# Keys of the next batch in cross attention: three context buffers, and the key sums ahead of a value product

## Chip, cores, metric

One core of a Trainium2 chip runs one launch of the kernel. The metric is the time of the device in microseconds (us), less is better. TensorE is called PE here, VectorE DVE, ScalarE ACT, GpSimd POOL, and SP is the engine that issues the transfers. PEld is the load of PE's weights.

## What is computed

A decoder layer with three parts, each followed by a layer norm, for 16 batches of 100 rows of 512: causal self attention with 16 heads, cross attention, and a routed feed-forward with two of eight experts. The change lies in the cross attention, whose computation is this (hidden is x, encoder is the context of 361 rows per batch):

```python
q = (hidden_states @ Wq + bq).reshape(b, s, 16, 128).transpose(0, 2, 1, 3)
k = (encoder_hidden_states @ Wk + bk).reshape(b, se, 4, 128).transpose(0, 2, 1, 3)
v = (encoder_hidden_states @ Wv + bv).reshape(b, se, 4, 128).transpose(0, 2, 1, 3)
q = _rmsnorm(q, qn_w)      # over the 128 of a head
k = _rmsnorm(k, kn_w)
scores = jnp.einsum('bhsd,bhed->bhse', q, k_of_its_group) / sqrt(128) + mask
out = softmax(scores) @ v_of_its_group
return out @ Wo
```

There are 16 query heads and 4 key and value heads, so 4 query heads share one key head.

## The kernel before

The kernel is written engine by engine: each engine has its own program of instructions in a fixed order, and semaphores tie them together (`wait_ge`, `then_inc`). Nothing is reordered by a scheduler. Three phases follow each other: self attention with the query projection, cross attention (`cross_attention_phase`), and the experts. All products are float32 products made of three float32r ones, high times high, high times low and low times high (`product3`, whose matmuls all carry line 75). An operand therefore has to be split: ACT copies it to the high half, and DVE or POOL subtracts that to get the low half.

The cross attention runs `body(j)` for batches j = 0 to 15 and then once more for what is left over. A batch has four groups s = 0 to 3, one per key head, and each engine walks through them. In group s PE does, for h = 0, 1, 2: the scores of query head h (3 matmuls, line 75, b_q with b_kTh and b_kTl), the transposes of one third of the probabilities of the group before (line 951), and a `quarter`, which is a piece of other work. Then come the scores of head 3, a fourth quarter, more pieces, and the product of the values with the probabilities of the group before (`values_product`). What the pieces are:

- Group 0: the output projection of the batch before, its third group of heads, as quarters (one query head each); the values of this batch (`values(j, 0)` ahead of the value product, 1 and 2 behind it).
- Group 1: the output projection of the batch before, its fourth group of heads, as quarters; then `keys(j + 1, 0)`, the first key head of the next batch. It waits for all three context pieces of that batch to be split (`ctx_lo`).
- Group 2: `keys` 1 and 2 in the quarters, `keys` 3 behind them, one head of the output projection; the value product; then `key_sums` (line 987), which sums the squares of the four key heads with a matrix of ones.
- Group 3: output projection in the quarters and around the value product.

The context of a batch is three pieces of 121 rows. SP loads each (`load_ctx`, line 863) to one of two raw buffers `ctxr[:, c % 2]`, so that the third waits for the low half of the first. ACT makes the high half (`context_hi`, line 1113) in group 1, one behind each of the first three exponents, and POOL the low half (`context_lo`, line 1404).

A key head goes through: DVE adds the bias (`key_bias`, line 1215), ACT squares (`key_square`, line 1094), PE sums, ACT takes logarithm, exponential and square (`key_root`, lines 1100 to 1104), DVE makes a Newton step (`key_newton`, lines 1221 and 1224), SP writes the four rows of roots to memory and loads them back spread over 128 partitions (`spread_key_roots`, lines 878 and 882, tensor b_krb), DVE scales (`key_scale`, line 1229), ACT and DVE split (lines 1108 and 1233). The root stands at the start of ACT's group 3, the Newton step behind the first probabilities in DVE's group 3, and the scaling of key head 0 in the middle of it:

```python
if now:
    queries(n + 1)
    if s == 3 and not last:
        key_scale(j + 1, 0)
    masked(j, s, 3)
    invert_sums(j, s, 0)
    if s == 3 and not last:
        keys_lo(j + 1, 0)
    invert_sums(j, s, 2)
```

`masked` (line 1250) reads the scores of a head and writes them with the mask and their maximum, ACT's `exponent` (line 1126) follows, and `invert_sums` (line 1256) releases POOL, which in `normalise` scales heads 0 and 1 of the group (line 1420, behind the small line 1399), makes the low half of the queries of the next group (`queries_lo`, line 1409), and scales heads 2 and 3. The first scores of a group wait for that low half (`q_lo`) and for the split key (`kt_lo`), its first transpose for all four scaled heads (`p_rdy`). Evictions to SBUF of the attention output are `b_oTh` (ACT, line 1190) and `b_oTl` (DVE, line 1326).

Keys have buffers for two batches of four heads (`[P, 2, XKV, SEP + 1]`), the squares share memory with the high halves and the raw keys with the low ones.

## Time and profile before

| what | value |
|---|---|
| median of 3 runs | 1666.06 us (1663.55 to 1667.65) |
| the profiled execution, its own time | 1665.94 us |
| span in its trace | 1663.6 us |
| PE busy | 1460.4 us (88%) |
| DVE, ACT, POOL busy | 855.6, 800.2, 509.1 us |

The profile is one execution. Its times are read as: start, duration, engine, line, operation, what is written and what is read, and in brackets how long the engine stood idle in front of it and what released it. A matmul's duration holds its passage through the array, so that matmuls behind each other start closer together than they last. "Granted clock" (PEclk) is the share of the full 2.4 GHz that PE was given; 0.50 is 1.2 GHz.

The cross attention fills the stretch from about 447 to 1446 us of the span.

### The profile page before, as it was taken

How to read it: one execution, taken by the hardware profiler on the slowest of the kernel's cores; microseconds unless marked ns; L12 is line 12 of the kernel's file. 1: busy time of each engine (PE TensorE's matmuls, PEld its weight loads, DVE VectorE, ACT ScalarE, POOL GpSimd, SP SyncE). 2: the span in 40 equal slices, each digit the busy share in tenths (PEclk: the TensorE clock that was granted, in tenths of full speed). 3: DMA queues.
4: the chain of work that ended last, by engine and by line, in shares of the span. 5: the costliest groups of instructions: out<-in, count | busy, mean ns of one | idle time of the engine just before them, and what ended most of it. 6: DMA issues, size and time to landing. Idle time of an engine off the chain costs nothing. (4 is left out here: it accounts for less than half of the span.)

```text
span 1663.6 us, 24851 instructions
## 1 busy us (share of the span) xinstructions
PE 1460.4 (88%) x8667; PEld 1237.8 (74%) x8667; DVE 855.6 (51%) x2739; ACT 800.2 (48%) x2074; POOL 509.1 (31%) x750
## 2 busy tenths in 40 slices
PE   7899999999977899898898898898898898669997
PEld 7688888777766787787787786786786787547874
DVE  2644444444465554555555555555554555554457
ACT  4555655554454544544444444444453454433346
POOL 1222212111032322332332332233233223563164
PEclk9999999999988999999899899899898998869999
DMA  5212202213342212212212212112212214175463
GB/s 180 81 31 70 71 32 70 70 33 111 102 157 83 60 52 61 75 43 56 76 42 61 70 41 71 61 41 73 64 37 76 65 33 132 42 242 179 148 205 130
DMA packets 79902, 138.27 MB, mean 83 GB/s; under 512 B 13056, under 2 KB 56484, under 8 KB 78884
## 3 DMA queue, kind: packets, MB, share of 16 engines
q1 hardware_dynamic: 75204, 121.75, 23.8%
q0 software_dynamic: 4576, 14.95, 3.2%
q8 instruction: 70, 1.15, 0.3%
q14 instruction: 52, 0.43, 0.1%
HBM read 105.12 MB, written 31.55 MB: 82 GB/s over the span
## 5 line engine op out<-in xcount | busy, mean ns | idle before, releaser
L75 PE MATMUL bank<-b_kTh,b_q 128*100 128x362 f32 x512 | 183.9, 360 | 66.4 <-POOL b_q L1409 56.9
L1399 POOL TENSOR_TENSOR b_pcarry<-b_half 128x1 f32<-128x1 f32 x128 | 37.4, 292 | 482.2 <-DVE b_rinv L1256 482.2
L1126 ACT ACTIVATE b_probs<-b_probs,b_nmax 100x361 f32<-100x361 f32 x256 | 151.7, 592 | 40.4 <-DVE b_nmax L1250 40.3
L1250 DVE CUSTOM_DVE_ANT_0 b_probs<-bank,b_mask 100x361 f32<-100x361 f32 x256 | 135.4, 529 | 62.8 <-issue 44.3
L75 PEld LDWEIGHTS bank<-b_kTh,b_q 128*100 128x100 f32 x512 | 92.3, 180 | 93.6 <-POOL b_q L1409 64.1
L1243 DVE TENSOR_TENSOR b_pTl<-bank,b_pTh 121x400 fp32r<-121x400 f32 x192 | 110.0, 573 | 79.7 <-ACT b_pTh L1121 78.3
L1121 ACT ACTIVATE b_pTh<-bank 121x400 fp32r<-121x400 f32 x192 | 95.5, 498 | 114.2 <-PE bank L951 113.3
L1420 POOL TENSOR_SCALAR b_probs<-b_probs,b_rinv 100x361 f32<-100x361 f32 x256 | 145.4, 580 | 0.0
L75 PE MATMUL bank<-b_ctxh,b_Wkh 128*128 128x362 f32 x256 | 95.2, 372 | 48.7 <-POOL b_ctxl L1404 48.7
L951 PEld LDWEIGHTS bank<-ident,b_probs 100*121 100x121 f32 x768 | 121.2, 209 | 18.7 <-POOL b_probs L1420 16.9
L951 PE MATMUL bank<-ident,b_probs 100*121 100x100 f32 x768 | 125.6, 291 | 10.7 <-POOL b_probs L1420 10.1
L75 PE MATMUL bank<-b_Woh,b_oTh 128*100 128x512 f32 x256 | 118.0, 461 | 1.4 <-DVE b_oTl L1326 1.4
L437 ACT ACTIVATE a_probs<-a_probs,a_nmax 100x100 f32<-100x100 f32 x256 | 93.2, 367 | 46.9 <-DVE a_nmax L559 46.8
L75 PE MATMUL bank<-b_Wol,b_oTh 128*100 128x512 f32 x256 | 107.5, 420 | 0.0
L75 PE MATMUL bank<-b_Woh,b_oTl 128*100 128x512 f32 x256 | 106.4, 416 | 0.0
L1404 POOL TENSOR_TENSOR b_ctxl<-b_ctxr,b_ctxh 128x484 fp32r<-128x484 f32 x45 | 51.1, 1135 | 170.1 <-ACT b_ctxh L1113 170.1
L1326 DVE SCALAR_TENSOR_TENSOR b_oTl<-bank,b_bv,b_oTh 128x400 fp32r<-128x400 f32 x64 | 40.4, 631 | 114.2 <-ACT b_oTh L1190 114.2
L75 PEld LDWEIGHTS bank<-b_ctxh,b_Wkh 128*128 128x128 f32 x256 | 51.6, 202 | 57.5 <-POOL b_ctxl L1404 55.5
L75 PE MATMUL bank<-a_x1Th,a_Wqh 128*128 128x400 f32 x256 | 91.8, 359 | 1.0 <-ACT a_qsx L461 0.7
L1409 POOL TENSOR_TENSOR b_q<-b_q_raw,b_q 128x400 fp32r<-128x400 f32 x64 | 81.5, 1274 | 30.8 <-ACT b_q L1132 30.8
L75 PE MATMUL bank<-b_ctxh,b_Wkl 128*128 128x362 f32 x256 | 90.1, 352 | 0.0
L75 PE MATMUL bank<-b_ctxl,b_Wkh 128*128 128x362 f32 x256 | 89.5, 350 | 0.0
(264 smaller groups left out, 3902.6 us busy)
## 6 DMA issues: line engine op xcount, KB each, us to landing
q_d<-a_qb SPq DMA_DIRECT2D x64, 200.0 KB, 2.5
b_q_raw<-q_d SPq DMA_DIRECT2D x64, 200.0 KB, 2.5
b_q_raw<-rs_d SPq DMA_DIRECT2D x64, 200.0 KB, 3.4
b_ctxr<-in_ctxT SPq DMA_DIRECT2D x48, 242.0 KB, 4.6
b_krb<-kr_d SPq DMA_DIRECT2D x64, 181.0 KB, 3.7
y_d<-c_y SPq DMA_DIRECT2D x32, 256.0 KB, 3.5
c_Eraw<-in_expert_w SPq DMA_DIRECT2D x10, 512.0 KB, 7.8
a_stage<-in_Wq SPq DMA_DIRECT2D x4, 1024.0 KB, 5.0
```

The source lines that it names most:

```text
L75: mm = eng.matmul(out, lhsT=l(c), rhs=r(c), start=first and k == 0, stop=last and k == n - 1)
L437: e = act.activation(probs[:, r, c, :], probs[:, r, c, :], ACT.Exp, scale=-1.0, bias=nmax[:, h:h + 1], accum_out=psums[:, r, c:c + 1])
L951: mm = pe.transpose(t_bank[c % 2][0:KT, h * S:(h + 1) * S], probs[:, s % 2, h, c * KT:(c + 1) * KT], ident_s[0:S, 0:S])
L1121: act.activation(pTh[:, c, :], t_bank[c % 2][0:KT, 0:XG * S], ACT.Copy).then_inc(pt_hi, 1)
L1126: act.activation(p, p, ACT.Exp, scale=-1.0, bias=nmax[:, s % 2, h:h + 1], accum_out=psums[:, s % 2, h:h + 1]).then_inc(e_rdy, 1)
L1243: dve.tensor_tensor(pTl[:, c, :], t_bank[c % 2][0:KT, 0:XG * S], pTh[:, c, :].bitcast(F32), ALU.subtract).then_inc(pt_lo, 1)
L1250: dve.tensor_tensor_reduce(out=probs[:, s % 2, h, 0:SE], in0=s_bank[h % 2][0:S, 0:SE], in1=mask_s[:], scale=-1.0, scalar=BIG, op0=ALU.add, ...
L1326: dve.scalar_tensor_tensor(out=oTl[:, kv, :], in0=o_bank[:, 0:XG * S], scalar=bv_s[:, kv:kv + 1], in1=oTh[:, kv, :].bitcast(F32), op0=ALU.add,
L1399: pool.tensor_tensor(pcarry[:, k:k + 1], half_s[:, 0:1], half_s[:, 0:1], ALU.add)
L1404: pool.tensor_tensor(ctxl[:, :, cols], ctxr[:, c % 2], ctxh[:, :, cols].bitcast(F32), ALU.subtract).then_inc(ctx_lo, 1)
L1409: pool.tensor_tensor(q_s[:, n % 2, 1], q_raw[:, n % 2, 1], q_s[:, n % 2, 0].bitcast(F32), ALU.subtract).then_inc(q_lo, 1)
L1420: pool.tensor_scalar(p, p, rinv[:, s % 2, h:h + 1], 1.0, ALU.mult, ALU.mult).then_inc(p_rdy, 1)
```

## The change

Three things are changed, all in the cross attention. First, `ctxr` has three buffers instead of two, a load each, all three at the start of a batch's program on SP; the high halves move to the end of group 0, each behind a value's high half, whose product `values(j, c)` was the last to read that piece's high half (in batch 0: behind the splits of weights). Second, `keys(j + 1, 1)` moves from group 2 to group 1, keys 2 and 3 take the quarters of group 2, and `key_sums` goes ahead of the value product with two heads of the output projection instead of one in front of it; the head comes out of group 3. ACT's root and DVE's Newton step move with it to the end of group 2, and scaling and splitting of key head 0 move to the end of group 3, behind both inversions. Third, the keys have five slots in a ring (`KS`) instead of eight, and `key_bias` waits for the scores that last read the slot. `a_gap` and `b_free` only keep addresses. The core of the diff (indexes changed from `jn % 2, kv` to `(XKV * jn + kv) % KS` alike everywhere else are left out):

```diff
@@ -45,6 +45,7 @@
 SEQ = SE + 1
+KS = XKV + 1
@@ -94,12 +95,12 @@
         Wkh, Wkl, Wvh, Wvl = [sb(f"b_{k}", [P, DC, D]) for k in ("Wkh", "Wkl", "Wvh", "Wvl")]
-        ctxr = sb("b_ctxr", [P, 2, DC, KT], F32)
+        ctxr = sb("b_ctxr", [P, KC, DC, KT], F32)
         ctxh, ctxl = sb("b_ctxh", [P, DC, SEP]), sb("b_ctxl", [P, DC, SEP])
...
     return Head(bank, bk_s, sem("b_bk_in"), Wkh, Wkl, Wvh, Wvl, ctxr, ctxh, ctxl, pieces, [sem("b_w_raw0"), sem("b_w_raw1")], sem("b_w_hi"), sem("b_w_lo"),
-                [sem("ctx_in0"), sem("ctx_in1")], sem("ctx_hi"), sem("ctx_lo"), sem("k_done"))
+                [sem(f"ctx_in{c}") for c in range(KC)], sem("ctx_hi"), sem("ctx_lo"), sem("k_done"))
@@ -255,8 +257,8 @@
             sp.wait_ge(qx_done, XH * (B // GB - 1))
-            for n in range(2):
-                sp.dma_start(head.ctxr[:, n], ctxT[n]).then_inc(head.ctx_in[n], 16)
+            for c in range(KC):
+                sp.dma_start(head.ctxr[:, c], ctxT[c]).then_inc(head.ctx_in[c], 16)
             for m in range(TAIL, NQ):
@@ -264,9 +266,6 @@
                         sp.dma_start(head_raw[:, n], head.pieces[2 + n][0]).then_inc(head.w_raw[n], 16)
-                if m == CTX_FRAME[0] + 3:
-                    sp.wait_ge(head.ctx_lo, 1)
-                    sp.dma_start(head.ctxr[:, 0], ctxT[2]).then_inc(head.ctx_in[0], 16)
             sp.wait_ge(x1_out, 16 * B)
@@ -769,19 +768,20 @@
             pass
-        with nc.sbuf_tensor("b_k_sq", [P, 2, XKV, SEP + 1], F32) as k_sq:
+        with nc.sbuf_tensor("b_k_sq", [P, KS, SEP + 1], F32) as k_sq:
             pass
-        kTh = sb("b_kTh", [P, 2, XKV, SEP + 1], F32R)
+        kTh = sb("b_kTh", [P, KS, SEP + 1], F32R)
         with nc.sbuf_tensor("b_above", [S, (B - 1) * E * E], F32) as above_s:
             pass
-        with nc.sbuf_tensor("b_k_raw", [P, 2, XKV, SEP + 1], F32) as k_raw:
+        with nc.sbuf_tensor("b_k_raw", [P, KS, SEP + 1], F32) as k_raw:
             pass
-        kTl = sb("b_kTl", [P, 2, XKV, SEP + 1], F32R)
+        kTl = sb("b_kTl", [P, KS, SEP + 1], F32R)
         Vh, Vl = sb("b_Vh", [KT, KC, XKV * XHD], F32R), sb("b_Vl", [KT, KC, XKV * XHD], F32R)
...
         oTh, oTl = sb("b_oTh", [P, XKV, XG * S], F32R), sb("b_oTl", [P, XKV, XG * S], F32R)
+        sb("b_free", [P, 2 * (2 * XKV - KS) * (SEP + 1) - DC * KT])
         x1_s, y_s = sb("b_x1", [S, D]), sb("b_y", [S, D])
@@ -846,21 +846,13 @@
-        def ctx_loads(jn, c):
-
-            return 16 * (jn + 1) if c == 1 else 16 * (2 * jn + 1 + c // 2)
-
         block = ctx.enter_context(nc.Block())
...
             def load_ctx(jn, c):
-                if c == 0:
-                    wait(sp, ctx_lo, 3 * jn)
-                if c == 2:
-                    sp.wait_ge(ctx_lo, 3 * jn + 1)
-                src = ctxT[bass.ds(KC * jn + c, 1)].rearrange("a p c t -> p (a c) t")
-                sp.dma_start(ctxr[:, c % 2], src).then_inc(ctx_in[c % 2], 16)
+                sp.wait_ge(ctx_lo, KC * (jn - 1) + c + 1)
+                sp.dma_start(ctxr[:, c], ctxT[KC * jn + c]).then_inc(ctx_in[c], 16)
@@ -894,14 +886,12 @@
                     if not last:
-                        load_ctx(j + 1, 0)
-                        load_ctx(j + 1, 1)
+                        for c in range(KC):
+                            load_ctx(j + 1, c)
                     load_q(4 * j + 2, 0, 16 * j + 4)
...
                         load_weights(KV_PIECES + 3)
-                    if not last:
-                        load_ctx(j + 1, 2)
                     if last:
@@ -1032,9 +1022,9 @@
                         if s == 2 and not last:
-                            keys(j + 1, 1 + q // 2, range(2 * (q % 2), 2 * (q % 2) + 2))
+                            keys(j + 1, 2 + q // 2, range(2 * (q % 2), 2 * (q % 2) + 2))
                         if s == 3:
-                            output(j, (q + 1) // XG, ((q + 1) % XG,))
+                            output(j, (q + 2) // XG, ((q + 2) % XG,))
@@ -1057,18 +1047,15 @@
                         keys(j + 1, 0)
+                        keys(j + 1, 1)
                     if s >= 2 and first:
...
                     if s == 2:
+                        output(j, 0, range(2))
                         if not last:
-                            keys(j + 1, 3)
-                        output(j, 0, range(1))
-                    if s == 3:
-                        output(j, 1, range(1, 2))
+                            key_sums(j + 1)
                     if before:
                         values_product(n - 1, (s + 3) % 4, j)
-                    if s == 2 and not last:
-                        key_sums(j + 1)
                     if s == 0 and now and not first:
@@ -1158,8 +1145,6 @@
                     n, before, now = 4 * j + s, not (first and s == 0), not past
-                    if s == 3 and not last:
-                        key_root(j + 1)
                     for h in range(3):
@@ -1167,23 +1152,23 @@
                             exponent(j, s, h)
-                        if s == 1 and not last:
-                            context_hi(j + 1, h)
                     if s == 2 and not last:
-                        key_square(j + 1, 1)
+                        key_square(j + 1, 2)
                     if now:
                         queries_hi(n + 1)
-                        if s == 3 and not last:
-                            keys_hi(j + 1, 0)
                         exponent(j, s, 3)
...
                         key_square(j + 1, 0)
+                        key_square(j + 1, 1)
                     if s == 2 and not last:
-                        key_square(j + 1, 2)
                         key_square(j + 1, 3)
+                        key_root(j + 1)
+                    if s == 0 and first:
+                        for c in range(KC):
+                            context_hi(1, c)
                     if before:
@@ -1195,9 +1180,12 @@
                             values_hi(j, c)
+                            if not last:
+                                context_hi(j + 1, c)
                     if s < 2 and now:
...
                     if s == 3 and not last:
+                        keys_hi(j + 1, 0)
                         keys_hi(j + 1, 1)
@@ -1212,11 +1200,12 @@
                 dve.wait_ge(k_done, XKV * jn + kv + 1)
-                dve.tensor_scalar(k_raw[:, jn % 2, kv, 0:SEQ], key_bank(jn, kv)[:, 0:SEQ], bk_s[:, kv:kv + 1], None,
+                wait(dve, s_done, XG * (XKV * jn + kv + 1 - KS))
+                dve.tensor_scalar(k_raw[:, (XKV * jn + kv) % KS, 0:SEQ], key_bank(jn, kv)[:, 0:SEQ], bk_s[:, kv:kv + 1], None,
                                   ALU.add).then_inc(k_ev, 1)
...
             def key_newton(jn):
-                t = k_sq[:, jn % 2, 0, 0:SEQ]
+                t = k_sq[:, XKV * jn % KS, 0:SEQ]
                 dve.wait_ge(k_rt, jn + 1)
@@ -1289,20 +1278,16 @@
                             probs_lo(n - 1, h)
-                        if s == 3 and h == 0 and not last:
-                            key_newton(j + 1)
                     if s == 0 and routed(j):
...
                     if s == 2 and not last:
-                        key_bias(j + 1, 1)
+                        key_bias(j + 1, 2)
                     if now:
                         queries(n + 1)
-                        if s == 3 and not last:
-                            key_scale(j + 1, 0)
                         masked(j, s, 3)
                         invert_sums(j, s, 0)
-                        if s == 3 and not last:
-                            keys_lo(j + 1, 0)
+                        if s == 2 and not last:
+                            key_bias(j + 1, 3)
                         invert_sums(j, s, 2)
@@ -1311,14 +1296,15 @@
                         key_bias(j + 1, 0)
+                        key_bias(j + 1, 1)
                     if s == 2 and not last:
-                        key_bias(j + 1, 2)
-                        key_bias(j + 1, 3)
+                        key_newton(j + 1)
                     if s == 3 and not first:
...
                     if s == 3 and not last:
+                        key_scale(j + 1, 0)
                         key_scale(j + 1, 1)
@@ -1332,6 +1318,7 @@
                     if s == 3 and not last:
+                        keys_lo(j + 1, 0)
                         keys_lo(j + 1, 1)
```

How it moves instructions. On DVE, in group 3 of a steady batch, before (line 1229 is a key's scaling, 1233 its low half, 1261 the queries):

```order
L1261 TENSOR_TENSOR b_q_raw<-b_q_raw 128x400
L1229 TENSOR_TENSOR b_k_raw<-b_k_raw,b_krb 128x362
L1249 MEMSET b_carry 100x1
L1250 ISA b_probs,b_nmax<-bank,b_mask 100x361
L1250 ISA b_nmax 100x1
L1256 RECIPROCAL b_rinv<-b_psums 100x2
L1233 TENSOR_TENSOR b_kTl<-b_k_raw,b_kTh 128x362
L1256 RECIPROCAL b_rinv<-b_psums 100x2
L1391 TENSOR_SCALAR b_y<-b_y,b_mv,b_rstd 100x512
L1229 TENSOR_TENSOR b_k_raw<-b_k_raw,b_krb 128x362
L1326 SCALAR_TENSOR_TENSOR b_oTl<-bank,b_bv,b_oTh 128x400
L1233 TENSOR_TENSOR b_kTl<-b_k_raw,b_kTh 128x362
```

and now (1218 is the scaling, 1222 the low half, 1250 the queries, 1245 the inversions, 1378 the norm, 1312 b_oTl):

```order
L1250 TENSOR_TENSOR b_q_raw<-b_q_raw 128x400
L1238 MEMSET b_carry 100x1
L1239 ISA b_probs,b_nmax<-bank,b_mask 100x361
L1239 ISA b_nmax 100x1
L1245 RECIPROCAL b_rinv<-b_psums 100x2 x2
L1378 TENSOR_SCALAR b_y<-b_y,b_mv,b_rstd 100x512
L1218 TENSOR_TENSOR b_k_raw<-b_k_raw,b_krb 128x362 x2
L1312 SCALAR_TENSOR_TENSOR b_oTl<-bank,b_bv,b_oTh 128x400
L1222 TENSOR_TENSOR b_kTl<-b_k_raw,b_kTh 128x362 x2
```

The scaling that stood between the queries and the last `masked` has gone behind both inversions and the norm, and the low half of key 0 behind b_oTl.

On ACT, at the end of group 0 and the start of group 1, before (1117 is a value's high half, 1113 a context piece's, 1126 an exponent):

```order
L1190 ACTIVATE b_oTh<-bank,b_bv 128x400
L1117 ACTIVATE b_Vh<-bank 121x512 x3
L1108 ACTIVATE b_kTh<-b_k_raw 128x362
L1121 ACTIVATE b_pTh<-bank 121x400
L1126 ACTIVATE b_probs,b_psums<-b_probs,b_nmax 100x361
L1113 ACTIVATE b_ctxh<-b_ctxr 128x4x121
L1121 ACTIVATE b_pTh<-bank 121x400
L1126 ACTIVATE b_probs,b_psums<-b_probs,b_nmax 100x361
L1113 ACTIVATE b_ctxh<-b_ctxr 128x4x121
L1121 ACTIVATE b_pTh<-bank 121x400
```

and now (1104 the value's high half, 1100 the context piece's, 1113 an exponent):

```order
L1100 ACTIVATE b_ctxh<-b_ctxr 128x4x121
L1104 ACTIVATE b_Vh<-bank 121x512
L1100 ACTIVATE b_ctxh<-b_ctxr 128x4x121
L1104 ACTIVATE b_Vh<-bank 121x512
L1100 ACTIVATE b_ctxh<-b_ctxr 128x4x121
L1095 ACTIVATE b_kTh<-b_k_raw 128x362
L1108 ACTIVATE b_pTh<-bank 121x400
L1113 ACTIVATE b_probs,b_psums<-b_probs,b_nmax 100x361
L1108 ACTIVATE b_pTh<-bank 121x400
L1113 ACTIVATE b_probs,b_psums<-b_probs,b_nmax 100x361
```

All three context splits are ahead of the group's first probabilities (b_pTh) now.

On PE, at the end of group 2, before (line 987 is key_sums):

```order
L75 MATMUL bank<-b_ctxl,b_Wkh 128x362
L75 MATMUL bank<-b_ctxh,b_Wkl 128x362
L75 MATMUL bank<-b_Woh,b_oTh 100x512
L75 MATMUL bank<-b_Wol,b_oTh 100x512
L75 MATMUL bank<-b_Woh,b_oTl 100x512
L75 MATMUL bank<-b_pTh,b_Vh 128x400
L75 MATMUL bank<-b_pTl,b_Vh 128x400
...
L75 MATMUL bank<-b_pTh,b_Vl 128x400
L987 MATMUL bank<-b_k_sq,b_ones 32x362 x4
L75 MATMUL bank<-b_kTh,b_q 100x362
```

and now (line 977 is key_sums):

```order
L76 MATMUL bank<-b_Woh,b_oTh 100x512
L76 MATMUL bank<-b_Wol,b_oTh 100x512
L76 MATMUL bank<-b_Woh,b_oTl 100x512
L977 MATMUL bank<-b_k_sq,b_ones 32x362 x4
L76 MATMUL bank<-b_pTh,b_Vh 128x400
L76 MATMUL bank<-b_pTl,b_Vh 128x400
L76 MATMUL bank<-b_pTh,b_Vl 128x400
```

The sums stand ahead of the nine matmuls of the value product (b_pTh, b_pTl, b_Vh, b_Vl) now, and a second output head (b_Woh, b_Wol) in front of them.

## Rows read from the trace of the kernel before

**Rows 1.** The waits over the whole run (line waiting <- releaser: us in total, times, longest us).

```profile
PE bank L75 <- POOL b_q L1409: 56.9, 17, 4.0
...
PE bank L75 <- POOL b_ctxl L1404: 48.7, 15, 5.1
...
DVE b_k_raw L1229 <- DMA b_krb<-kr_d: 38.3, 15, 2.9
...
PE bank L951 <- POOL b_probs L1420: 10.1, 16, 1.2
```

**Rows 2.** The timeline of PE in batch 6 (of 0 to 15): start us, us, [idle before <-releaser].

```profile
855.50 0.43 PE L75 MATMUL bank<-b_ctxh,b_Wkh 128*128 128x362 f32 x1 [3.07 <-POOL b_ctxl L1404]
...
886.87 0.41 PE L75 MATMUL bank<-b_kTh,b_q 128*100 128x362 f32 x1 [3.74 <-POOL b_q L1409]
```

**Rows 3.** The timelines of SP's queue, ACT and POOL, third context piece.

```profile
851.00 0.33 SPq L863 DMA_DIRECT2D b_ctxr<-in_ctxT  x1
846.50 0.60 ACT L1117 ACTIVATE b_Vh<-bank 121x512 fp32r<-121x512 f32 x1 [2.21 <-PE bank L75]
...
853.64 0.61 ACT L1113 ACTIVATE b_ctxh<-b_ctxr 128x484 fp32r<-128x484 f32 x1 [1.38 <-DMA b_ctxr<-in_ctxT]
854.33 1.12 POOL L1404 TENSOR_TENSOR b_ctxl<-b_ctxr,b_ctxh 128x484 fp32r<-128x484 f32 x1 [1.80 <-ACT b_ctxh L1113]
```

**Rows 4.** The timeline of DVE in the fourth group of the same batch.

```profile
876.52 0.54 DVE L1224 SCALAR_TENSOR_TENSOR b_krs<-b_k_sq,b_krs 128x362 f32<-128x362 f32 x1
...
882.39 0.54 DVE L1229 TENSOR_TENSOR b_k_raw<-b_k_raw,b_krb 128x362 f32<-128x362 f32 x1 [2.67 <-DMA b_krb<-kr_d]
...
883.31 0.16 DVE L1256 RECIPROCAL b_rinv<-b_psums 100x2 f32<-100x2 f32 x1
...
884.23 1.25 DVE L1391 TENSOR_SCALAR b_y<-b_y,b_mv,b_rstd 100x512 f32<-100x512 f32 x1
885.40 0.52 DVE L1229 TENSOR_TENSOR b_k_raw<-b_k_raw,b_krb 128x362 f32<-128x362 f32 x1
885.85 0.62 DVE L1326 SCALAR_TENSOR_TENSOR b_oTl<-bank,b_bv,b_oTh 128x400 fp32r<-128x400 f32 x1
```

**Rows 5.** The timeline of POOL, end of the same group.

```profile
885.14 1.67 POOL L1409 TENSOR_TENSOR b_q<-b_q_raw,b_q 128x400 fp32r<-128x400 f32 x1
...
887.24 1.10 POOL L1420 TENSOR_SCALAR b_probs<-b_probs,b_rinv 100x361 f32<-100x361 f32 x2
```

**Rows 6.** Stretches of the run: PE, PEld, DVE, ACT, POOL busy, then PEclk, DMA share, GB/s.

```profile
856.68:860.09 3.41, 3.41 (x13) 3.39 (x12) 1.35 (x5) 0.56 (x1) 2.25 (x5) 0.50 0.23 65
887.40:894.23 6.83, 6.12 (x23) 4.90 (x22) 2.15 (x8) 2.12 (x6) 0.94 (x2) 0.50 0.48 140
505.11:508.52 3.41, 3.41 (x13) 2.92 (x13) 1.86 (x7) 2.57 (x6) 0.00 (x0) 0.50 0.02 5
1529.11:1532.52 3.41, 3.41 (x12) 2.73 (x11) 1.29 (x2) 0.28 (x1) 2.95 (x3) 0.50 0.48 149
304.80:312.00 7.20, 7.20 (x50) 7.16 (x51) 1.33 (x3) 2.93 (x13) 1.71 (x2) 1.00 0.18 68
```

**Rows 7.** The timeline of PE, idle times of 1.8 to 2.4 us elsewhere.

```profile
304.72 1.45 PE L287 MATMUL bank<-a_xTr,a_wk 128*128 128x200 f32 x7 [2.35 <-DMA a_xTr<-in_xT]
...
504.14 0.82 PE L987 MATMUL bank<-b_k_sq,b_ones 128*32 128x362 f32 x8 [2.01 <-ACT b_k_sq L1094]
...
1527.56 0.50 PE L1678 MATMUL bank<-Esplit,c_xgh 128*128 x1 [1.79 <-DVE c_xgl L1872]
```

**Rows 8.** The timelines of PE, DVE and ACT at the last key's square (third group).

```profile
870.05 0.39 PE L75 MATMUL bank<-b_Woh,b_oTh 128*100 128x512 f32 x1
...
870.73 0.34 PE L75 MATMUL bank<-b_pTh,b_Vh 121*128 121x400 f32 x1
...
870.25 0.60 DVE L1215 TENSOR_SCALAR b_k_raw<-bank,bk 128x362 f32<-128x362 f32 x1 [0.56 <-PE bank L75]
870.88 0.56 ACT L1094 ACTIVATE b_k_sq<-bank,bk 128x362 f32<-128x362 f32 x1 [0.59 <-DVE b_k_raw L1215]
```

33 lines of the change are left out of this document (17 added, 16 removed).

## Prediction

> **What bounds the kernel now.** The page gives PE the largest busy share, so I read first who PE waits for [rows 1]. Two waits in the cross attention carry nearly all of it. For the low half of a context piece PE stands 48.7 us in 15 waits, one per batch that prepares a next one, 3.25 us each. For the low half of the queries it stands 56.9 us in 17 waits; 14 of them are at the start of a steady batch, such as the 3.74 us one of [rows 2], and behind it the first transpose waits again for POOL's scaled probabilities, 10.1 us in 16 waits, 0.6 us each. Nobody else's idle time matters unless it ends in one of these.
>
> Second, what ends each wait. The context: the third piece's load is issued at 851.00, because it shares a buffer with the first, ACT waits 1.38 us for it, copies in 0.61 us, POOL subtracts in 1.12 us, and PE starts at 855.50 [rows 2, 3]. The queries: DVE waits 2.67 us for the key roots that come back from memory (38.3 us in 15 waits over the run), and the last mask, both inversions and so POOL's whole round stand behind that wait [rows 1, 4]. POOL's low half of the queries ends at 885.14 + 1.67 = 886.81, and PE starts at 886.87 [rows 2, 5]. So the query wait is really a wait of DVE for a round trip of the keys through memory: 877.06 (end of the Newton step) to 882.39, 5.3 us [rows 4].
>
> Third, the clock. Each of the two waits is followed by a stretch at a granted clock of 0.50, that is 1.2 GHz instead of 2.4: 3.41 us behind the context wait, 6.83 us behind the query wait, with PE busy 3.41 and 6.12 us in them [rows 6]. Work at half the clock takes twice as long, so half of the busy time is lost: 1.7 and 3.1 us per batch. The same two stretches follow in each of the 14 steady batches.
>
> **The change, part by part.**
>
> *A. Context pieces.* The loads leave with the batch's first ones and the copies stand behind the value evictions. Today the last value copy starts at 846.50 and takes 0.60 us [rows 3]; the last context copy then ends near 847.10 + 0.61 = 847.7 and POOL's subtraction near 848.9. POOL is free there: it waits for the context today too. PE wants the piece at 855.50 - 3.07 = 852.43, so 3.5 us are to spare and the wait goes: 15 x 3.25 = 49 us, and the slow stretch behind it, 15 x 1.7 = 26 us. Sum 74 us with the rounding. That a whole context load is not there in time I exclude: it is issued over a group earlier than the copy.
>
> *B. The query wait.* The roots now start a value product earlier and the scaling stands last, so DVE's 2.67 us wait and the 0.46 us of the scaling (882.39 to the next operation) leave the path of the last mask: everything from it on comes 3.1 us earlier. What is late next has two branches. POOL: the low half of the queries ends at 883.7 instead of 886.81, the second pair of probabilities at 887.24 + 1.10 - 3.1 = 885.2 [rows 5]. DVE: the norm moves from 884.23 to about 881.1 and takes 1.25 us, two scalings 0.52 us each, b_oTl 0.62 us, the low half of the key as much as a scaling, 0.52 us: 884.5 [rows 4]. Before, that low half was ready long ahead; now the first scores of the next batch wait for it. PE arrives at 886.87 - 3.74 = 883.13 less one output head that has moved to the third group (870.05 to 870.73, 0.68 us [rows 8]): 882.45. So PE waits 2.1 us for the key and then 0.2 us at most for the probabilities. The group itself starts a little easier for ACT, whose three root operations leave its head, while b_oTl of the group before is later by the Newton step (both are inside DVE's idle time). I take 2.0 us of waiting in place of 3.7 + 0.6 = 4.3: 14 x 2.3 = 32 us. Ends: 1.2 us of waiting if POOL's subtraction and the norm run less against each other (the first branch's 883.7 is 1.25 us behind 882.45, and then only the queries' low half is late), 3.0 us if one of them is held for another 1 us.
>
> That last end has a row: POOL's low half took 1.67 us while DVE ran norm, scaling and b_oTl beside it, and the scaling stayed at 0.52 us [rows 4, 5]; so here POOL paid. The Trainium skill ("SBUF — State Buffer", Who interferes with whom) says that a DVE operation with two SBUF inputs and a GpSimd operation that reads SBUF exclude each other for a whole instruction. The trace agrees in kind (no row here shows a full block). The rule speaks against this change, since two scalings now stand back to back beside POOL's subtraction: by it the later one would wait out 1.1 us more, and the sum would be 14 x 1.1 = 15 us smaller. I keep 2.0 us, as the row has the contention in it already.
>
> *C. The slow stretch behind that wait.* Does a wait of 2.0 us still bring it? The trace has two such waits with 3.41 us at 0.50 behind them, of 2.01 us (before 504.14) and of 1.79 us (before 1527.56), and one without, of 2.35 us (304.80 to 312.00 is at 1.00) [rows 6, 7]. So mostly yes, but for one stretch of 3.41 us rather than two, since the second wait at the transpose is gone: a loss of 1.7 us in place of 3.1. With it staying away in a few batches I take 1.6 us gained, 14 x 1.6 = 22 us. Ends: 1.4 (always) and 3.1 (never).
>
> *D. New waits.* The sums now stand directly behind two output heads. Today the last key's matmuls end at 870.05, its bias runs 870.25 to 870.85, its square 870.88 to 871.44 [rows 8]: 1.4 us, and two heads cover 2 x 0.68 = 1.36 us. But the last exponent of the group shares ACT and the last mask DVE; I take 0.3 us of waiting, between 0 and the 2.01 us that the same line waited in the first batch [rows 7]. The third context copy stands ahead of ACT's first probabilities of group 1, so the third transpose, which needs that bank, can be late by up to its 0.6 us; I take 0.25. Together 15 x 0.55 = 8 us lost. The root ahead of b_oTh delays nothing that PE reaches in the next 3 us. The second key in group 1 and the ring of five slots cost nothing: each key's bias waits for scores that are one group old, and PE's matmuls are the same in number.
>
> **Sum**: 74 + 32 + 22 - 8 = 120 us. The profiled execution took 1665.9 us, as good as the median of 1666.1, so 1546 us. The likeliest case's own range: all low ends, 74 + 14 x 1.3 + 14 x 1.4 - 15 x 1.2 = 94 us, are 1572; all high ends, 76 + 14 x 3.1 + 14 x 3.1 - 1 = 162 us, are 1504.
>
> **Rivals.**
>
> *The clock stays up.* The remaining wait is short enough, or broken in two, that no slow stretch follows. For it: the 2.35 us wait without one [rows 6, 7]. Against: the 1.79 and 2.01 us ones. A, D and a short wait of 1.3 us as above, C at 3.1: 74 + 42 + 43 - 3 = 156 us, 1510 us. Chance 0.18.
>
> *The key takes the query's place.* DVE is in order: norm, two scalings, b_oTl and the low half follow each other, and if the second scaling or b_oTl is held the first scores wait as long as today. For it: the branch of 884.5 is already the later one, and POOL and DVE stretch each other. Then B and C give nothing: 74 - 8 = 66 us, 1600 us. Chance 0.14.
>
> *The sums stop PE, slower.* One place, `key_sums` ahead of the value product: PE is in order, so while it waits for the last square, the value product waits, with it b_oTh, b_oTl and the scores of the next group. If the bias came late (DVE has it behind the last mask and an inversion that waits for ACT) the wait would cost itself and a slow stretch of 1.7 us. It has to pass 120 / 15 = 8 us per batch, so a wait of over 6.3 us, to make the kernel slower; at 8 us it would be 1546 + 15 x 9.7 = 1691 us. Only the first batch shows any such wait, of 2.01 us. Chance 0.03.
>
> *It does not do what it says.* If SP still issued the context loads late (they stand in order behind a load that waits for the batch's last scores) and another transfer kept the roots from returning earlier, nothing moves: 1666 us. The loads stand at the head of the batch today already, so 0.03.
>
> **How the numbers follow.** Forecast 0.62 (1504 to 1572), clock stays up 0.18, key takes the place 0.14, the sums 0.03, nothing 0.03. From 1500 to 1595 lie the forecast, the second case and the near part of the third: some 0.82. A measurement of this kernel tells about 0.3% (5 us) from no change; faster by more than that is the sum of the first three, 0.94, within it 0.03, slower 0.03.
>
> **What would show it.** A is right if PE no longer waits for b_ctxl and the 3.41 us stretch behind it is gone; B if DVE's wait for b_krb is gone and PE's wait at the batch's start is about 2 us, released by b_kTl or b_q; C by the number and length of stretches at 0.50, one per batch and 3.41 us long; D by PE's wait at the sums (about 0.3 us) and at b_probs' third transpose. A steady batch shorter by 8 us is the whole. The forecast is wrong if the sums wait over 1 us in every batch, if the start-of-batch wait stays above 3 us, or if PE's matmuls grow longer outside the slow stretches.

## The result, and the profile after

| what | before | after |
|---|---|---|
| median of 4 runs each, same chip | 1664.80 us (1663.20 to 1667.65) | 1538.93 us (1537.07 to 1541.84) |
| the profiled execution, its own time | 1665.94 us | 1541.84 us |
| span in its trace | 1663.6 us | 1539.9 us |

The ratio is 0.9244, 95% interval 0.9222 to 0.9266: the change takes 7.6% off, 126 us. The forecast of 1546 us was 7 us too high, inside its own range.

The page of after: busy time of each engine, and PE's granted clock in 40 slices.

```profile
PE 1411.1 (92%) x8667; PEld 1192.5 (77%) x8667; DVE 855.1 (56%) x2739; ACT 801.2 (52%) x2074; POOL 514.7 (33%) x750
...
PEclk9999999999998899999999999999999999689998
```

No engine does less: DVE, ACT and POOL are busy as long as before, within 6 us. PE has 49 us less of busy time with the same matmuls, since fewer of them run at 1.2 GHz; everything else that went is idle time of PE. Its waits over the whole run (as in [rows 1]):

```profile
PE bank L76 <- POOL b_q L1396: 20.9, 16, 3.1
PE bank L941 <- POOL b_probs L1407: 11.9, 16, 1.4
...
PE bank L76 <- DVE b_kTl L1222: 11.2, 2, 8.2
...
PE bank L941 <- DVE b_pTl L1232: 5.8, 15, 1.0
PE bank L977 <- ACT b_k_sq L1081: 5.8, 2, 4.0
```

The row of b_ctxl is gone (it was 48.7 us), that of b_q fell from 56.9 to 20.9 us, and the waits of line 977, the sums, are two in all, both in batch 0 (3.98 and 1.82 us), as before. The row of b_probs is no smaller (10.1 us before). The 8.2 us on b_kTl end batch 0, where PE waited 6.5 us for b_Wol before; b_pTl in 15 places is new. DVE has no wait for b_krb left (it was 38.3 us).

The same place in the batch as in [rows 2, 4, 5], here at the end of batch 7: PE at the start of batch 8 and at its first transpose, then DVE, then POOL. The first line is the one that [rows 2] leave out, PE's first transpose before.

```profile
888.39 1.14 PE L951 MATMUL bank<-ident,b_probs 100*121 100x100 f32 x4 [0.71 <-POOL b_probs L1420]
```

```profile
887.67 0.38 PE L76 MATMUL bank<-b_kTh,b_q 128*100 128x362 f32 x1 [1.25 <-POOL b_q L1396]
889.05 0.67 PE L941 MATMUL bank<-ident,b_probs 100*121 100x100 f32 x4 [0.67 <-POOL b_probs L1407]
```

```profile
884.39 0.17 DVE L1245 RECIPROCAL b_rinv<-b_psums 100x2 f32<-100x2 f32 x1 [0.68 <-ACT b_probs L1113]
884.47 0.92 DVE L1378 TENSOR_SCALAR b_y<-b_y,b_mv,b_rstd 100x512 f32<-100x512 f32 x1
885.31 0.97 DVE L1218 TENSOR_TENSOR b_k_raw<-b_k_raw,b_krb 128x362 f32<-128x362 f32 x2
886.21 0.62 DVE L1312 SCALAR_TENSOR_TENSOR b_oTl<-bank,b_bv,b_oTh 128x400 fp32r<-128x400 f32 x1
886.75 1.27 DVE L1222 TENSOR_TENSOR b_kTl<-b_k_raw,b_kTh 128x362 fp32r<-128x362 f32 x2
```

```profile
885.03 2.14 POOL L1396 TENSOR_TENSOR b_q<-b_q_raw,b_q 128x400 fp32r<-128x400 f32 x1
887.13 0.49 POOL L1386 TENSOR_TENSOR b_pcarry<-b_half 128x1 f32<-128x1 f32 x1
887.60 1.40 POOL L1407 TENSOR_SCALAR b_probs<-b_probs,b_rinv 100x361 f32<-100x361 f32 x2
```

None of these DVE rows waits for b_krb. The round trip of the roots is hidden: Newton's last step ends at 878.57, the scalings start at 885.31. PE's two waits, of 3.74 and 0.71 us, are now 1.25 and 0.67 us: what went is nearly all in the first. The first is put down to b_q, but POOL's low half of the queries ended at 887.17, half a microsecond ahead of PE's start; the first of the two low halves of the keys (b_kTl; it took 0.82 of the pair's 1.27 us) ended at 887.57, 0.10 us ahead. The experiment q_first decides which it was.

Where the time went, in three stretches (the 16 batches start at the row of the sums of batch 0; the steady one goes from the start of batch 1 to that of batch 15; the columns are those of [rows 6]). Before, and then after:

```profile
450.19:522.85 72.66, 52.67 (x267) 44.37 (x267) 41.95 (x102) 36.76 (x78) 25.35 (x32) 0.85 0.36 117
522.85:1378.77 855.92, 752.89 (x3965) 647.44 (x3965) 455.52 (x1388) 401.54 (x980) 275.49 (x460) 0.92 0.21 59
1378.77:1663.60 284.83, 235.67 (x1164) 186.29 (x1164) 153.84 (x354) 124.55 (x241) 126.42 (x137) 0.90 0.48 155
```

```profile
449.80:518.63 68.83, 51.23 (x268) 43.21 (x268) 45.64 (x104) 37.18 (x79) 24.27 (x32) 0.85 0.39 124
518.63:1259.15 740.52, 708.93 (x3964) 606.77 (x3965) 451.71 (x1386) 402.11 (x979) 281.55 (x461) 0.98 0.25 68
1259.15:1539.90 280.75, 231.30 (x1164) 182.81 (x1164) 153.77 (x354) 124.50 (x241) 126.09 (x136) 0.91 0.49 156
```

The 14 steady batches went from 61.14 to 52.90 us each, 115.4 us in sum: PE's idle time there from 103.0 to 31.6 us (length less busy), which is 71.4 us, and its busy time from 752.9 to 708.9 us, which is 44.0 us, with the granted clock at 0.98 instead of 0.92. The first batch gave 3.8 us and the rest of the run 4.1 us.

Before, 3.41 us at a clock of 0.50 stood behind the context wait and 6.83 us behind the query wait of a steady batch (the context wait of batch 1 had none). After, one stretch of 3.41 us stands behind the starts of batches 4, 6, 8, 10, 12 and 14 (six of the 13 starts inside the steady stretch), for example

```profile
889.84:893.25 3.41, 3.41 (x15) 3.00 (x14) 1.11 (x4) 1.08 (x4) 0.00 (x0) 0.50 0.53 199
```

and the next at 995.65; behind the start at 941.44 there is none.

### The profile page after: what moved, and what is told of

Read it like the earlier page. It is cut to its first block and busy times, and to the rows that moved or that the text cites. A ratio compares the mean times of both kernels' runs of the same rounds, so it can differ in the third digit from the quotient of the medians.

```text
span 1539.9 us, 24910 instructions
## 1 busy us (share of the span) xinstructions
PE 1411.1 (92%) x8667; PEld 1192.5 (77%) x8667; DVE 855.1 (56%) x2739; ACT 801.2 (52%) x2074; POOL 514.7 (33%) x750
## 5 line engine op out<-in xcount | busy, mean ns | idle before, releaser
L76 PE MATMUL bank<-b_kTh,b_q 128*100 128x362 f32 x512 | 177.3, 347 | 34.7 <-POOL b_q L1396 20.9
L941 PE MATMUL bank<-ident,b_probs 100*121 100x100 f32 x768 | 115.9, 275 | 17.7 <-POOL b_probs L1407 11.9
L941 PEld LDWEIGHTS bank<-ident,b_probs 100*121 100x121 f32 x768 | 109.9, 191 | 28.7 <-POOL b_probs L1407 17.6
L76 PE MATMUL bank<-b_Woh,b_oTh 128*100 128x512 f32 x256 | 111.5, 436 | 1.4 <-DVE b_oTl L1312 1.4
L599 DVE TENSOR_SCALAR a_qb<-bank,a_bq,a_qkw 128x400 f32<-128x400 f32 x64 | 44.3, 692 | 85.5 <-PE bank L76 85.4
L76 PE MATMUL bank<-a_x1Tl,a_Wqh 128*128 128x400 f32 x256 | 88.3, 345 | 0.0
L76 PE MATMUL bank<-a_x1Th,a_Wql 128*128 128x400 f32 x256 | 88.2, 345 | 0.0
L76 PE MATMUL bank<-b_ctxh,b_Wkh 128*128 128x362 f32 x256 | 88.0, 344 | 0.0
L76 PE MATMUL bank<-b_kTl,b_q 128*100 128x362 f32 x256 | 86.4, 337 | 0.0
L76 PE MATMUL bank<-b_ctxl,b_Wkh 128*128 128x362 f32 x256 | 84.1, 328 | 0.0
```

The source lines that it names most:

```text
L76: mm = eng.matmul(out, lhsT=l(c), rhs=r(c), start=first and k == 0, stop=last and k == n - 1)
L599: dve.tensor_scalar(qb[:, u % 2, :, m % XG, :], q_bank(m)[:, 0:GT].rearrange("p (b t) -> p b t", b=GB), bq_s[:, m % XH:m % XH + 1], qkw_s[ ...
L941: mm = pe.transpose(t_bank[c % 2][0:KT, h * S:(h + 1) * S], probs[:, s % 2, h, c * KT:(c + 1) * KT], ident_s[0:S, 0:S])
```

## The experiments

Each time is a median, with the ratio to the kernel before on the same chip; the change's own ratio is 0.9244.

### Which part brings what

**ctx_scale**: the change, with the keys, their sums, roots and Newton step back in the order of before (on the ring of five slots). The contexts and the place of the scaling stay as changed. Of the diff, PE's part:

```diff
-                            keys(j + 1, 2 + q // 2, range(2 * (q % 2), 2 * (q % 2) + 2))
+                            keys(j + 1, 1 + q // 2, range(2 * (q % 2), 2 * (q % 2) + 2))
...
                         keys(j + 1, 0)
-                        keys(j + 1, 1)
...
-                        output(j, 0, range(2))
                         if not last:
-                            key_sums(j + 1)
+                            keys(j + 1, 3)
+                        output(j, 0, range(1))
                     if before:
                         values_product(n - 1, (s + 3) % 4, j)
+                    if s == 2 and not last:
+                        key_sums(j + 1)
```

> The changed kernel with the keys' order of before: one key head in group 1, three in group 2, key_sums behind the value product, root and Newton step in group 3; the three context buffers, the early context splits and the late place of the scaling and low half of key 0 stay. Theory 1 (the place of the scaling frees the path, the place of the sums hardly matters): DVE reaches the scaling some 8.0 to 9 us after the group's start, the roots land 9.2 us after it, so 0 to 1.2 us of waiting per batch, 1540 to 1556 us. Theory 2 (the earlier sums and roots are what removes the wait): the query wait comes back, 14 x 3.9 = 54 us, about 1593 us.

Measured 1553.27 us, 0.9327 (0.9298 to 0.9356). So moving keys and sums, the largest part of the diff, is worth some 14 us of 126. In the steady batches it is worth 0.1 us each (52.99 against 52.90): DVE waits only 5.0 us in 13 places for the roots there. The steady stretch, and PE's waits in it (530 to 1262 us, which has 13 of the 14 starts here):

```profile
527.78:1269.66 741.88, 705.11 (x3964) 602.57 (x3965) 461.15 (x1386) 403.41 (x979) 278.04 (x462) 0.99 0.24 68
```

```profile
PE bank L76 <- issue: 23.8, 13, 2.2
PE bank L941 <- POOL b_probs L1411: 5.7, 14, 0.4
```

PE's idle time is 36.8 us there (length less busy) against 31.6 in the change: a later start of a batch (1.8 us on average), nothing at its first transpose, and 0.41 us at the first transpose of group 2. There the change has no wait, with a second key in group 1 ahead of it. Three stretches at half clock instead of six give most of that back. Between the two profiled executions lie 10.4 us, and 6.4 of them are in the first batch, 75.2 us long here and 68.8 in the change: one transpose waits 2.87 us (1.43 in the change) and the batch's end 9.68 us (8.18). The steady batches hold 1.4 us, and 2.8 us stand ahead of the cross attention, where the two kernels are the same.

**ctx_only**: ctx_scale, with the scaling, high half and low half of key 0 back in the middle of group 3. Only the contexts are as changed.

```diff
                         queries(n + 1)
+                        if s == 3 and not last:
+                            key_scale(j + 1, 0)
                         masked(j, s, 3)
                         invert_sums(j, s, 0)
+                        if s == 3 and not last:
+                            keys_lo(j + 1, 0)
...
-                        key_scale(j + 1, 0)
                         key_scale(j + 1, 1)
...
-                        keys_lo(j + 1, 0)
                         keys_lo(j + 1, 1)
```

> The context part alone (keys, sums and scaling in the order of before, on the ring of five slots). Theory 1 (the two waits are independent): the gain is 14 x (3.1 + 1.7) = 67 us and some 4 in the first batch, 1665 - 71 = 1594 us, with the 6.83 us slow stretches still there. Rival (with the context wait gone another engine is late in group 1 or 3, and the query wait grows): over 1610 us.

Measured 1620.40 us, 0.9722 (0.9695 to 0.9749): 46 us, less than expected for the contexts alone. The waits that are left inside the steady batches (these rows of waits, like those above and below, are of 530 to 1262 us unless said otherwise), and the steady stretch:

```profile
PE bank L76 <- POOL b_q L1403: 43.9, 12, 3.9
PE bank L941 <- POOL b_probs L1414: 11.6, 25, 0.7
PE bank L941 <- DVE b_pTl L1237: 4.5, 13, 0.4
```

```profile
524.94:1334.86 809.92, 740.50 (x3964) 626.79 (x3964) 461.82 (x1388) 402.75 (x980) 279.76 (x460) 0.94 0.23 62
```

The context wait of 3.1 us is gone, but 25 transposes wait for probabilities instead of 12 in the same window before (the new ones in group 2, 0.41 us each), and the third transpose of group 1 waits 0.35 us. PE's idle time falls from 103.0 to 69.4 us, 2.4 us per batch; its busy time from 752.9 to 740.5, 0.9 us per batch where I had counted 1.7 for the stretch at half clock. Together 3.3 us, the 46 us.

**scale_only**: the kernel before, with nothing changed but that place of the scaling.

```diff
                         queries(n + 1)
-                        if s == 3 and not last:
-                            key_scale(j + 1, 0)
                         masked(j, s, 3)
                         invert_sums(j, s, 0)
-                        if s == 3 and not last:
-                            keys_lo(j + 1, 0)
                         invert_sums(j, s, 2)
...
+                        key_scale(j + 1, 0)
                         key_scale(j + 1, 1)
...
+                        keys_lo(j + 1, 0)
                         keys_lo(j + 1, 1)
```

> The kernel before with nothing but the scaling and low half of key 0 moved behind both inversions and the norm. Theory 1: the query wait falls from 4.3 to about 2 us and its slow stretch to at most 3.41 us, 14 x (2.3 + 1.4 to 3.1) = 52 to 76 us, 1590 to 1613 us; the context wait of 3.1 us stays. Theory 2 (sums needed): at most 0.5 us per batch, 1655 us or more.

Measured 1595.21 us, 0.9564 (0.9530 to 0.9599): 71 us from three moved instructions (with the high half on ACT), with roots that come no earlier than before.

```profile
PE bank L75 <- POOL b_ctxl L1401: 39.8, 13, 3.4
PE bank L75 <- issue: 24.4, 13, 2.2
```

```profile
527.02:1318.85 791.83, 722.70 (x3964) 628.00 (x3965) 455.39 (x1386) 402.06 (x979) 273.46 (x462) 0.95 0.22 64
```

```profile
DVE b_k_raw L1228 <- DMA b_krb<-kr_d: 4.8, 13, 0.6
```

DVE still waits for the round trip (the last row, of the whole run), 0.4 us each time instead of 2.6, but behind both inversions, so POOL's round no longer hangs on it. PE's start of a batch waits 1.65 to 2.2 us in place of 3.7, and its first transpose not at all. The parts add up, nearly: 46 + 71 = 117 against 113 for ctx_scale.

**ctx_late_split**: the change, with the high halves of the context back in group 1, so that only the third buffer and the early loads are left of that part.

```diff
                             exponent(j, s, h)
+                        if s == 1 and not last:
+                            context_hi(j + 1, h)
...
                             values_hi(j, c)
-                            if not last:
-                                context_hi(j + 1, c)
```

> The changed kernel, but the context's high halves are back in group 1, one behind each exponent; the three buffers and early loads stay. Theory 1 (both the buffer and the place count): ACT's third copy starts near 852.3 instead of 853.64 of the trace before, POOL ends 1.4 us earlier, PE still waits 1.7 us per batch, with a slow stretch in some: 1538.9 + 15 x 1.7 + 0 to 25 = 1564 to 1590 us. Rival (the third buffer alone removes the wait): 1540 us. Other rival (only the place counts): 1538.9 + 15 x 3.1 + 25 = 1611 us.

Measured 1566.60 us, 0.9399 (0.9369 to 0.9429). PE waits again for the third piece, half as long as before:

```profile
PE bank L76 <- POOL b_ctxl L1388: 22.0, 14, 1.6
```

So the third buffer without the early copies takes about half of that wait, and the copies the rest. The early copies without the buffer were not run. A steady batch is 54.56 us long, 1.7 more than in the change: 1.57 us are this wait, 0.35 us at the third transpose are gone, and a stretch at 0.50 now follows every start of a batch and not every second one.

### What ends the wait that is left

K is the theory that the key's low half, last in DVE's chain, ends the wait at the batch's start; Q, that the queries' low half on POOL does, as the profile's releaser says.

**q_first**: POOL makes the queries' low half ahead of its first two probabilities in group 3.

```diff
+                if s == 3:
+                    queries_lo(n + 1)
                 for h in range(XG):
-                    if h == 2:
+                    if h == 2 and s != 3:
                         queries_lo(n + 1)
```

> The changed kernel, with POOL making the low half of the next queries ahead of the first pair of probabilities in group 3 (it stands idle there until the first inversion). In the changed kernel PE's start-of-batch wait ended at 887.67, while POOL's low half of the queries ended at 887.18 and DVE's low half of key 0 at 887.57. Theory K (the key's low half ends the wait, POOL's last pair the second one): the first wait shrinks by 0.3 us (less contention), the second of 0.67 us goes: 14 x 1.0 = 14 us and up to 12 us of slow stretches, 1513 to 1527 us. Theory Q (the query's low half ends the wait, as the profile labels it): both waits go, 14 x 1.9 + 12 = 39 us, 1500 us.

Measured 1543.75 us, 0.9283 (0.9259 to 0.9308): no gain, if anything a loss. PE, DVE and POOL at the start of batch 3:

```profile
623.41 0.38 PE L76 MATMUL bank<-b_kTh,b_q 128*100 128x362 f32 x1 [0.71 <-issue]
625.40 0.67 PE L941 MATMUL bank<-ident,b_probs 100*121 100x100 f32 x4 [1.28 <-POOL b_probs L1409]
```

```profile
620.74 0.68 DVE L1378 TENSOR_SCALAR b_y<-b_y,b_mv,b_rstd 100x512 f32<-100x512 f32 x1
...
622.78 0.97 DVE L1222 TENSOR_TENSOR b_kTl<-b_k_raw,b_kTh 128x362 fp32r<-128x362 f32 x2
```

```profile
620.09 1.05 POOL L1396 TENSOR_TENSOR b_q<-b_q_raw,b_q 128x400 fp32r<-128x400 f32 x1 [5.76 <-ACT b_q L1119]
621.10 1.27 POOL L1386 TENSOR_TENSOR b_pcarry<-b_half 128x1 f32<-128x1 f32 x1
622.34 1.76 POOL L1409 TENSOR_SCALAR b_probs<-b_probs,b_rinv 100x361 f32<-100x361 f32 x2
```

The queries' low half ends at 621.14, 2.3 us before PE starts at 623.41. So it doesn't end this wait; the first low half of a key, about half way through the pair that starts at 622.78, does. K is right on that, and the label b_q of the change's rows named the last but one. But both theories' times were too low. K had POOL's second pair of probabilities there in time, and it isn't: the carry, an operation on one column that takes 0.19 us in other places, takes 1.27 us beside DVE's norm and scalings, and the first pair of probabilities 1.76 instead of 1.11. POOL ends its round at 625.3, and the first transpose waits 1.28 us instead of 0.67. The sum of the two waits stays: 1.99 against 1.91 us.

**norm_last**: DVE's norm goes behind the low halves of the keys, to the place of a wait for the store of its rows; that wait moves to where the rows are written again (not shown).

```diff
-                    if s == 3 and not first:
-                        apply_norm(j - 1)
...
                     if s == 3 and not first:
-                        dve.wait_ge(x2_out, 16 * j)
+                        apply_norm(j - 1)
```

> The changed kernel, with the norm of group 3 on DVE behind the low halves of the keys instead of ahead of the scalings (and the wait for the store of the rows moved to where they are written again). The key comes about 0.9 us earlier. Theory K: the wait for the scores falls from 1.24 to about 0.8 us, where the query's low half is next, and the second wait grows by as much, since POOL's last pair still ends near 889.0: no change in time, 1535 to 1541 us. Theory Q: the first wait stays at 1.24 us, no change either; the two differ in that wait alone.

Measured 1540.80 us, 0.9258 (0.9232 to 0.9283). At the same place on DVE:

```profile
620.42 2.33 DVE L1218 TENSOR_TENSOR b_k_raw<-b_k_raw,b_krb 128x362 f32<-128x362 f32 x2
```

The two scalings take 2.33 us instead of 0.97, now that they lie beside POOL's low half of the queries, which in turn takes 1.39 us here and 2.14 in the change. The key's low half gains 0.8 us from the norm that no longer stands ahead of it and loses 1.4 us to the longer scalings. One wait of 1.47 us is left in place of two, and a steady batch is 52.24 us long, 9.2 us less in 14. But the stretch from the start of batch 15 to the end takes 288.4 us instead of 280.8, since the last norm is now late: a wait at line 998 that the change does not have (the row is of the whole run).

```profile
PE bank L998 <- DVE b_y L1377: 8.0, 1, 8.0
```

So most of the gain in the steady batches goes at the end of the run, where the old place of this one norm was not tried. In the median norm_last can't be told from the change.

**q_norm**: both edits.

> Both edits together: the low half of the queries first on POOL, the norm last on DVE. Theory K: the key is ready near 886.5 and PE's first wait is gone or under 0.3 us, POOL's last pair ends near 887.6 and the second wait is about 0.6 us: 14 x 1.3 = 18 us and up to 12 us of slow stretches, 1509 to 1521 us. Theory Q: no more than the query edit alone brings.

Measured 1541.80 us, 0.9271 (0.9249 to 0.9293): waits of 0.74 and 0.83 us, a steady batch of 52.23 us, the same 8.0 us at the end. K's forecast of 1509 to 1521 us did not come true: the waits that it had at 0.3 us or less and at 0.6 us are both longer.

**key_late**: two memsets of 0.46 us on DVE in free memory ahead of the low halves of the keys.

```diff
+                        dve.memset(free[:, 0:480], 0.0)
+                        dve.memset(free[:, 480:960], 0.0)
                         keys_lo(j + 1, 0)
```

> The changed kernel with two fills of 480 columns of unused memory on DVE ahead of the low half of key 0, about 0.5 us each. The first wait becomes about 2.2 us in one piece instead of 1.24 and 0.67 us with scores between them; POOL's last pair is then there. If the slow stretch follows the sum of the idle time: time up by 14 x 0.3 = 4 us and slow stretches in half of the batches as now, 1541 to 1546 us. If an unbroken wait brings it more often: one in each batch, 12 us more, 1550 to 1558 us. If the query's low half ended the wait so far (theory Q), the first wait would grow by only 0.6 us.

Measured 1555.44 us, 0.9347 (0.9323 to 0.9372).

```profile
898.50 0.38 PE L76 MATMUL bank<-b_kTh,b_q 128*100 128x362 f32 x1 [1.91 <-issue]
899.79 0.45 PE L941 MATMUL bank<-ident,b_probs 100*121 100x100 f32 x2 [0.58 <-POOL b_probs L1409]
```

The wait at the start grows from 1.24 to 1.91 us, that at the transpose shrinks by 0.09, and a steady batch is 1.1 us longer, the rest of it from more stretches at half clock. It was not the one unbroken wait that I wanted, so whether such a wait brings the stretch more often stays open. What is put into DVE's chain delays the scores, which is K once more, now from the other side; POOL's queries weren't touched.

### What more can be had

These runs were on another chip (before: 1673.43 us), where the stretch from the start of batch 15 to the end takes about 8 us longer (288.2 us in third_later's trace, 280.8 in the change's); the ratios are what compares.

**third_later**: the high half of the third context piece goes back to group 1, behind the first exponent, except in batch 0.

```diff
                             exponent(j, s, h)
+                        if s == 1 and h == 0 and not first and not last:
+                            context_hi(j + 1, KC - 1)
...
-                            if not last:
+                            if not last and c < KC - 1:
                                 context_hi(j + 1, c)
```

> The changed kernel, with the third context piece's high half moved behind the first exponent of group 1 (steady batches). The wait of 0.35 us at the third transpose of group 1 is put down to this copy standing ahead of ACT's first probabilities. If so it goes in 14 batches, 5 us less, 1534 us, and POOL's last context piece still ends over 2 us before PE wants it. Rival (the wait comes from the copies of key 2's high half, there before too): no change, 1539 us.

Measured 1529.71 us, 0.9141 (0.9122 to 0.9160), 1.1% below the change, where I had looked for a third of that. The waits, and the steady stretch:

```profile
PE bank L76 <- POOL b_q L1398: 16.1, 13, 1.2
PE bank L941 <- POOL b_probs L1409: 8.8, 13, 0.7
```

```profile
517.93:1235.08 717.15, 691.15 (x3965) 599.85 (x3965) 443.95 (x1386) 403.59 (x979) 282.23 (x461) 1.00 0.26 70
```

The 0.35 us wait for b_pTl is gone (PE's idle time 26.0 us instead of 31.6), as meant. And the waits at the starts are what they were, 1.24 and 0.67 us, but no stretch at half clock follows any of them: the granted clock is 1.00 over the 14 batches, and PE's busy time 17.8 us less. The chip alone does not do this: in weights_first, on the same chip and without this edit, such stretches stand behind seven of the 13 starts.

**weights_first**: in batch 0 the last two loads of the output projection's weights go ahead of the round trip of the roots on SP.

```diff
                     load_q(4 * j + 4, 0, 16 * j + 12)
+                    if first:
+                        load_weights(KV_PIECES + 6)
+                        load_weights(KV_PIECES + 7)
                     spread_key_roots(j + 1)
...
-                    load_weights(KV_PIECES + 6)
-                    load_weights(KV_PIECES + 7)
```

> The changed kernel, with the last two weight loads of the first batch ahead of the spreading of the key roots on SP. In the first batch PE waits 8.18 us at the start of batch 1; ACT waits there 4.56 us for the weights. Theory: the first batch is bound by these loads, which are issued at 506.4 though their buffer is free near 500.4; 4 to 6 us less, once, 1533 to 1535 us. Rival (the roots, delayed by the loads, are then as late): 1539 us.

Measured 1548.17 us, 0.9254 (0.9230 to 0.9279). The first batch is 3.8 us shorter in the trace (65.06 us; its last wait 4.29 us instead of 8.18), so the place of these loads made about half of that wait; in the median of the whole run it can't be told from the change.

**group3**: q_first, and DVE's norm in group 2, key 0 scaled between the two inversions, and its low half right behind the second one; the high half on ACT and POOL's root for the norm move forward with them.

> The changed kernel with the end of group 3 relieved: the norm and POOL's root for it in group 2, ahead of the Newton step, the low half of the queries first on POOL, and key 0 scaled and split around the second inversion. Theory (what is left of the start-of-batch wait is POOL and DVE holding each other up, so that work has to leave this place rather than change its order): the key is ready before PE comes, POOL's round of some 3.7 us undisturbed ends 0.4 to 1.4 us sooner: 14 x 0.4 to 1.4 = 6 to 20 us and 0 to 12 us of slow stretches, 1507 to 1533 us. Rival (POOL's round ends no sooner whatever stands on DVE, as in the three reorderings before): 1539 us or slower.

Measured 1540.15 us, 0.9209 (0.9191 to 0.9228), 0.4% below the change by the ratios, whose intervals overlap. PE hardly waits for the scores at a batch's start any more; the wait has gone to the first transpose:

```profile
PE bank L941 <- POOL b_probs L1412: 20.7, 14, 1.7
```

**best**: group3, third_later and weights_first together.

> All three of this call together. If they are independent, the sum of their gains: 1495 to 1525 us.

Measured 1522.86 us, 0.9107 (0.9086 to 0.9128), 1.5% below the change by the ratios; from third_later alone it can't be told.

```profile
PE bank L942 <- POOL b_probs L1415: 23.0, 15, 1.7
```

```profile
513.55:1229.52 715.97, 695.36 (x3965) 605.17 (x3965) 451.56 (x1387) 403.44 (x980) 277.85 (x458) 0.99 0.23 71
```

Its steady batches are 51.1 us long, third_later's 51.2: idle time fell from 26.0 to 20.6 us, and three stretches at half clock came back behind the one longer wait. What it has over third_later in the traces is mostly in the first batch, 63.9 us long instead of 68.8. The change and four other orders of the same work on DVE and POOL left 1.5 to 2.0 us of waiting per batch, and none less.

## Why the prediction was right, point by point

The sum was 120 us, and the two profiled executions differ by 124. For the steady batches I had 14 x (3.25 + 1.7 + 2.3 + 1.6 - 0.55) = 116 us, and measured 115.4. In idle time of PE that was 5.0 us per batch by the terms and 5.1 measured; in the clock 3.3 and 3.1. So the two sides of the sum are right, and inside them some terms were off.

**A, the context wait.** Right in its mechanism and its idle time: the wait is gone, in all batches. ctx_late_split shows what I had not split, that the third buffer without the early copies takes only half of it. The clock part was too large: alone, the contexts gave back 0.9 us per batch, not 1.7. One reason is a wrong reading: I wrote that the slow stretch follows the context wait in each of the 14 steady batches, and it does in 13. Behind the wait of 2.97 us at 550.86, in batch 1, the kernel before has none:

```profile
548.00:580.00 32.00, 26.14 (x155) 23.26 (x155) 19.21 (x61) 16.61 (x40) 11.52 (x21) 1.00 0.22 60
```

That accounts for 1.7 us of the sum; the rest of the shortfall is that a slow stretch cost less than half of its length, which stays unexplained (see the last section). And the 15th time, in the first batch, brought 3.8 us in all and not the 4.9 - 0.55 of the terms. The context wait there was 5.06 us, but a transpose now waits 1.43 us, and PE runs into the weights sooner: the wait at the batch's end grew from 6.48 to 8.18 us. I had multiplied by 15 without looking at what the first batch waits for next.

**B, the query wait.** 1.24 + 0.67 = 1.91 us are left, and I took 2.0, on the branch of the key. q_first and key_late show that branch right. The times at which I had it, 2.1 us and then at most 0.2, were not: the key came 0.9 us sooner than that, and POOL's round later, because POOL's low half took 2.14 us and not 1.67. The two misses cancel, which was luck. By the Trainium skill's rule on the SBUF ("SBUF — State Buffer", Who interferes with whom) the second scaling would have waited out 1.1 us. The rows show the 1.1 us, but on the other side: POOL's subtraction took 2.14 us where it takes 1.05 without them, and both scalings ran at 0.97 together. As the key and not the queries ended PE's first wait, that can have cost at most the 0.67 us at the transpose, 14 x 0.67 = 9 us in the sum and not 15 (an estimate).

What I had not seen is how much of B belongs to the one moved scaling. I wrote that the roots start a value product earlier *and* the scaling stands last; scale_only shows that the second alone is worth 71 us, and ctx_scale that, with the contexts changed too, the first adds 0.1 us per steady batch.

**C, the slow stretch behind it.** Mostly yes, I wrote, one per batch; it was six in 14 batches, behind starts with the same two waits as the others. In scale_only PE's busy time over the steady batches is 30.2 us less than before, 2.2 us per batch, where I had 1.6. As the contexts' part of the clock was smaller and this one larger, the sum of both came out right by luck. The rival in which the clock stays up (1510 us) was wrong for the change, but third_later has its condition, a steady stretch at full clock, with the very same waits at the starts.

**D, new waits.** At the sums none in steady batches (I took 0.3 us), with two output heads ahead of them. At the third transpose 0.35 us (I took 0.25). The rival in which the sums stop PE was wrong with that, and the one in which the key holds the first scores as long as today too: it ends the wait, but at 1.24 us.

## What to carry to other kernels

Look at what stands in front of an in-order engine's wait for a transfer, and at what stands behind it: here the cheapest cure for a round trip through memory was to move the waiting instruction behind everything that others need, and three moved instructions gave more than half of the gain. Where a wait has several semaphores, take the releaser's end time and subtract it from the waiter's start: in these traces the cause ended 0.1 us ahead, and the engine that was named but did not cause the wait 0.5 us or more. And where two engines slow each other down, putting one's work earlier can move the loss from one wait to the next, as in q_first and group3; count both waits, and try the order on the chip.
